# Scatter-adding expert rows straight into the output, and the order of the last block in a graph and mixture-of-experts layer

## The chip, the cores and the metric

The kernel runs on one NeuronCore of a Trainium2 chip. The metric is the device time of one execution in microseconds (us), given as the median of several runs. A core has a matrix engine (TensorE, PE in the profile, with its weight loads shown as PEld), a vector engine (DVE), a scalar engine (ACT), GpSimd (POOL) and a sync engine (SP) that here only issues DMAs. They run their own instruction streams and meet at semaphores. SBUF is the on-chip memory, PSUM holds matrix results.

## The reference

The layer takes 3125 nodes with 256 features and 50,000 edges. Its steps are:

```
xn  = layernorm(x)
gate = sigmoid(silu(edge_attr @ W1 + b1) @ W2 + b2)          # per edge
aggr = segment_sum(gate * xn[src], dst)                       # per node
x1  = x + xn + silu([xn, aggr] @ U1 + c1) @ U2 + c2 + linear_attention(xn)
probs = softmax(layernorm(x1) @ gate_w + gate_b)              # 16 experts
top 2 experts a node, weights divided by their sum
out = x1 + sum over a node's 2 experts e of
        weight * (silu(xn2 @ w1[e]) * (xn2 @ w2[e])) @ w3[e]  # xn2 = layernorm(x1), hidden 512
```

All tensors are float32. The change touches only the last line: the sum of the expert results onto `x1`.

## The kernel before

The first 797 us compute `x1` (kept in SBUF as tile `x`) and the routing. The rest is the expert stage. The 6250 pairs of node and expert are sorted into blocks of 256 slots, each block with one expert (`SB = 256`, at most `CAPB = 40` blocks). How many blocks there are is known only at run time. With this input there are 32, numbered 0 to 31, so `end`, read by `last_pair`, is 15. The 32 blocks have 8192 slots, and 1942 of them hold no pair. Such a spare slot has a destination row from `NP` = 3200 on, which is past the 3125 rows of the output.

Matrix products are done to nearly full float32 precision by splitting each operand into a high and a low half and adding three products (`PARTS`). ACT makes the high half (`w_high` for weights, `hid_high` for the hidden layer), DVE the low half (`w_low`, `hidden_low`). `ws[r]` holds both halves of weight `r`: 0 and 1 are the two column halves of w1 and w2 together, 2 is w3. There is one such pair for each `r`, so a new block's weights can be split only after the matrix engine has finished with the old ones. The raw weights have two buffers (`wst[r][p]`, with `p` the parity of the block), which SP fills in `load_w`.

For block `i` the work is:

- POOL gathers 256 rows of `xn2` (`gather_slots`, L648, two indirect DMAs of 128 rows);
- PE transposes them (`turn`), and computes the first layer in two halves: `expert_up(i, p, 0)` and `expert_up(i, p, 1)` (L1755, 24 matmuls each);
- for each half ACT applies silu (`silu_g`), DVE multiplies (`hidden`, L1442), ACT copies the high half (`hid_high`, L890), DVE makes the low half (`hidden_low`);
- PE computes the second layer, `expert_down(i, p)` (L1767, 24 matmuls);
- ACT scales by the slot weight and copies to `ys[p]` (`copy_y`, L897, two halves; it raises `s_y`);
- POOL adds the rows to a DRAM array (`scatter_slots`): it copies the block's destination rows to `idx[p]` (L657) and issues two indirect DMAs with `compute_op=ALU.add` (L661, 128 rows each). Since two blocks may hold the same node, a block's scatter waits until the one before has landed (`s_yst[1 - p]`).

The scatters go to `acc_d` (`out_rows` in the profile), with 3200 rows for nodes and 256 for spare slots. SP stores `x1` there in five chunks as its tiles are made, and one more copy that initializes the 256 spare rows. At the very end SP waits for all scatters and copies 3125 rows from `acc_d` to the output (L483).

The order on PE is software-pipelined by hand. In the loop, the first layer of the next block stands between the first and second layer of this one, and loop passes for pairs that don't exist are skipped by `If`. After the loop, blocks 30 and 31 remain in part. PE runs these three steps after the first half of block 31's first layer: second layer of 30, second half of the first layer of 31, second layer of 31. ACT and DVE follow the same order in their `block_steps`. POOL gathers four blocks ahead of its scatters, and after its loop four scatters remain (blocks 28 to 31).

Of the kernel before, what the change touches and what calls it, by code (L numbers as in the profile page):

```python
# [20 lines left out]
f32 = mybir.dt.float32  # L21
# [3 lines left out]
ALU = mybir.AluOpType  # L25
# [3 lines left out]
P = 128  # L29
N, D, E, RB = 3125, 256, 50000, 64  # L30
DC = D // P
NT = -(-N // P)
NP = NT * P
LAST = N - (NT - 1) * P
# [12 lines left out]
SB = 256  # L47
# [27 lines left out]
def ds(start, size):  # L75
    return bass.ds(start, size)
# [29 lines left out]
def gps_layer(nc, x_d, src_d, dst_d, first_d, rbf_d, W1_d, b1_d, W2_d, b2_d, U1_d, c1_d, U2_d, c2_d,  # L106
# [2 lines left out]
    XW = D + 2  # L109
    xn2_d = nc.dram_tensor("xn2_rows", (NP, XW), f32).ap()  # L110

    acc_d = nc.dram_tensor("out_rows", (NP + SB, D), f32).ap()

    ctx = ExitStack()
    with ctx:
# [32 lines left out]
        x = sb("x_nodes", [P, NT, D])  # L148
# [44 lines left out]
        ws = [[part(fr, 1024 * (2 * r + k), 4, D) for k in range(2)] for r in range(3)]  # L193
# [16 lines left out]
        idx = [sb(f"idx{i}", [P, ET], i32) for i in range(2)]  # L210
# [50 lines left out]
        dest = part(hgx, 128 + NS, NS).bitcast(i32)  # L261
# [7 lines left out]
        wst = [[part(big, 1024 * (2 * r + i), 4, D) for i in range(2)] for r in range(3)]  # L269
# [5 lines left out]
        ys = [part(xfl, 3072 + 512 * i, 2, D) for i in range(2)]  # L275
# [42 lines left out]
        s_turn = sem("gather_turn")  # L318
# [60 lines left out]
        s_acc = sem("x1_stored")  # L379
# [8 lines left out]
        def _(sp):  # L388
# [52 lines left out]
            for v in range(NB):  # L441
                for t in range(*XN2AT.get(v, (0, 0))):
                    store_xn2(t)
                for t0, end in CHUNKS:
                    if (end - 1) // 2 == v:
                        sp.wait_ge(s_x1, v + 3)
                        sp.dma_start(acc_d[t0 * P:end * P, :].rearrange("(t p) d -> p t d", p=P), x[:, t0:end, :])\
                            .then_inc(s_acc, 16)
                        if t0 == 0:
                            sp.dma_start(acc_d[NP:, :].rearrange("(t p) d -> p t d", p=P), x[:, 0:SB // P, :])\  # L450
                                .then_inc(s_acc, 16)
            for t in range(*CHUNKS[-1]):
                store_xn2(t)

# [25 lines left out]

            for p in range(2):
                sp.wait_ge(s_yst[p], 32 * end + 32)
            sp.dma_start(out_d[:, :], acc_d[0:N, :]).then_inc(s_out, 16)  # L483
            sp.wait_ge(s_out, 16)


        @block.gpsimd
        def _(pool):
# [161 lines left out]


            def scatter_slots(i, jp, p):
                pool.wait_ge(s_y, i + 3)
                if not (type(i) is int and i == 0):
                    pool.wait_ge(s_yst[1 - p], (jp + p) * 32)
                pool.wait_ge(s_tabi, 2)
                pool.tensor_copy(idx[p][:, 2:4], dest[:, ds(i * 2, 2)]).then_inc(s_didx, 1)  # L657
                pool.wait_ge(s_tabi, 2)
                pool.wait_ge(s_didx, i + 3)
                for s in range(2):  # L660
                    pool.indirect_dma_start(acc_d[:, :], bass.IndirectOffsetOnAxis(idx[p][:, 2 + s:3 + s], 0),  # L661
                                            ys[p][:, s, :], None, compute_op=ALU.add).then_inc(s_yst[p], 16)
            pool.sem_inc(s_didx, 2)
            for i in range(4):
                gather_slots(i, i % 2)
# [19 lines left out]
        def _(act):  # L685
# [184 lines left out]
            def w_high(r, i, j, p, first=False):  # L870
                act.wait_ge(s_win[r][p], (j + 1) * (32 if r < 2 else 16))

                if not first:
                    act.wait_ge(*((s_h, i * 4 + 4 + 2 * r + 2) if r < 2 else (s_o, i + 2)))
                act.copy(ws[r][0], wst[r][p]).then_inc(s_wh[r], 1)  # L875
# [11 lines left out]
            def hid_high(i, p, q):  # L887
                act.wait_ge(s_hid, i * 2 + q + 3)
                act.wait_ge(s_o, i + 1)
                act.copy(hids[p][0][:, 2 * q:2 * q + 2, :], hidf[q]).then_inc(s_hdh, 1)  # L890
# [8 lines left out]
                last.then_inc(s_y, 1)  # L899


            def block_steps(i, j, p, jn, last=False):
                silu_g(i, 0)
                if not last:
                    w_high(0, i + 1, jn, 1 - p)
                    slots_high(i + 1, 1 - p)
                hid_high(i, p, 0)
                w_high(2, i, j, p, first=(type(i) is int and i == 0))
                if not (type(i) is int and i == 0):
                    copy_y(i - 1, jn - 1, 1 - p)  # L910
                silu_g(i, 1)
                hid_high(i, p, 1)
                if not last:
                    w_high(1, i + 1, jn, 1 - p)
# [19 lines left out]
        def _(dve):  # L934
# [486 lines left out]

            dve.sem_inc(s_hid, 2)
            dve.sem_inc(s_xlo, 1)
            def w_low(r, i, p):
                dve.wait_ge(s_wh[r], i + 1)
                dve.tensor_tensor(ws[r][1], wst[r][p], ws[r][0].bitcast(f32), ALU.subtract).then_inc(s_wlo[r], 1)  # L1426

            def slots_low(i, p):
                dve.wait_ge(s_xhi, i + 1)
# [21 lines left out]
            def block_steps(i, p, last=False):  # L1451
                hidden(i, p, 0)
                if not last:
                    w_low(0, i + 1, 1 - p)
                    slots_low(i + 1, 1 - p)
                    slot_weights(i + 1, 1 - p)
                hidden_low(i, p, 0)
                w_low(2, i, p)
                hidden(i, p, 1)
                hidden_low(i, p, 1)  # L1460
                if not last:
                    w_low(1, i + 1, 1 - p)
# [19 lines left out]
        def _(pe):  # L1482
# [263 lines left out]
            def expert_up(i, p, q):  # L1746
                pe.wait_ge(s_wlo[q], i + 1)
                pe.wait_ge(s_xlo, i + 2)

                pe.wait_ge(s_hid, i * 2 + q + 1)  # L1750
                for m in range(2):
                    for k in range(2):
                        for c in range(DC):
                            for a, b in PARTS:
                                last = mm(ps[:, 2 * m + q, k * SB:(k + 1) * SB],  # L1755
                                          ws[q][a][:, 2 * m + c, k * P:(k + 1) * P], xTs[p][b][:, c, :],
                                          start=c == 0 and (a, b) == PARTS[0], stop=c == DC - 1 and (a, b) == PARTS[-1])
                    last.then_inc(s_h, 1)

            def expert_down(i, p):  # L1760
                pe.wait_ge(s_wlo[2], i + 1)
                pe.wait_ge(s_hdl, i * 2 + 2)
                pe.wait_ge(s_y, i + 1)
                for s in range(2):
                    for k in range(HC):
                        for a, b in PARTS:
                            last = mm(ps[:, 4 + p, s * D:(s + 1) * D], hids[p][a][:, k, s * P:(s + 1) * P],  # L1767
                                      ws[2][b][:, k, :],
                                      start=k == 0 and (a, b) == PARTS[0], stop=k == HC - 1 and (a, b) == PARTS[-1])
                last.then_inc(s_o, 1)  # L1770
            turn(0, 0, 0)
# [5 lines left out]
            with pe.Fori(0, CAPB // 2 - 1) as j:  # L1777
                with pe.If(end > j):
# [6 lines left out]
                    expert_down(j * 2 + 1, 1)  # L1785
                    expert_up(j * 2 + 2, 0, 1)
            expert_up(end * 2 + 1, 1, 0)
            expert_down(end * 2, 0)
            expert_up(end * 2 + 1, 1, 1)
            expert_down(end * 2 + 1, 1)  # L1790


# [35 lines left out]
```

## Time and profile before

| What | Value |
| --- | --- |
| median of 3 runs | 1130.9 us (1129.13 to 1131.05) |
| the profiled execution: its own time | 1130.0 us |
| its span, from first to last instruction | 1128.2 us |
| mean granted TensorE clock, as a share of full speed | 0.957 |
| chain of waits over the whole span, largest shares | POOL 39%, PE 37% |
| busy share of PE, DVE, ACT, POOL | 92%, 79%, 61%, 66% |
| expert stage, from the first first-layer matmul | 809.8 us to the end |

The profile page gives busy time by engine, the span in slices, the DMA queues, the chain of work that ended last, and groups of instructions by line. Times are from the start of the span. A row of a timeline has the start, the duration, engine and line, operation, what it writes `<-` what it reads, and in brackets the idle time of its engine before it with what ended that idle time. A DMA issued by POOL is shown for the time in which POOL generates it. When its data has landed is told apart, as time "to landing" from the start of the issue. SPq is SP's queue.

### The profile page before, as it was taken

The numbers are of one execution on the slowest core, as the hardware profiler recorded it, in microseconds if no ns is written. First come the engines' busy times: TensorE is split into PE (matmuls) and PEld (weight loads), VectorE is DVE, ScalarE is ACT, GpSimd is POOL, SyncE is SP. The second block draws the span as 40 slices with busy tenths as digits, with TensorE's granted clock in tenths as the row PEclk, the third lists the DMA queues.
The fourth block names the chain that finished last, engine by engine and source line by source line (L and its number), as shares of the span: only waits on it lengthen the run. The fifth ranks groups of instructions, "written<-read, shape, count | busy, mean of one in ns | idle before, by whom it ended". The sixth has DMA issues, their size and how long they took to land.

```text
span 1128.2 us, 23398 instructions
## 1 busy us (share of the span) xinstructions
PE 1033.9 (92%) x7884; PEld 978.0 (87%) x7884; DVE 889.9 (79%) x1411; ACT 686.0 (61%) x1055; POOL 746.6 (66%) x703
## 2 busy tenths in 40 slices
PE   4897999999999999999999999983499999999992
PEld 2466899999999999999999989983399999999991
DVE  7877998888999888888888843688487777777760
ACT  2562767766666666666666635652266777767760
POOL 5447877777777777777777756510267777767752
PEclk9998999999999999999999999985599999999996
DMA  7211444444444444444444401230678999888855
GB/s 241 77 53 42 135 146 143 143 141 141 143 143 142 140 141 141 143 143 141 141 141 143 125 26 56 85 104 1 178 215 226 230 235 226 237 233 235 227 119 137
DMA packets 118921, 165.25 MB, mean 146 GB/s; under 512 B 18625, under 2 KB 91382, under 8 KB 118774
## 3 DMA queue, kind: packets, MB, share of 16 engines
q1 hardware_dynamic: 87174, 95.14, 26.1%
q0 software_dynamic: 31104, 68.26, 25.3%
q8 instruction: 48, 0.79, 0.3%
q10 hardware_dynamic: 560, 0.79, 0.2%
q14 instruction: 35, 0.29, 0.1%
HBM read 145.62 MB, written 21.71 MB: 148 GB/s over the span
## 4 chain that ended last, share of the span: by engine, by line
POOL 39%; PE 37%; issue 13%; DVE 7%; DMA 2%; ACT 0%; POOLq 0%; DVEq 0%; ACTq 0%; SPq 0%
POOL big L590 19%; POOL hgx L590 19%; PE ps L1755 16%; PE ps L1767 8%; PE ps L1629 3%; PE ps L1502 2%; PE ps L1641 2%; PE ps L1654 2%; PE ps L1742 1%; PE ps L1668 1%; DVE st L961 1%; PE ps L1511 1%; PE ps L1512 1%; DMA hgx<-xn_rows,hgx 1%; PE ps L1495 1%
## 5 line engine op out<-in xcount | busy, mean ns | idle before, releaser
L1574 PE MATMUL ps<-fr 128*128 128x256 f32 x2352 | 306.9, 287 | 3.2 <-DVE fr L1023 3.2
L1574 PEld LDWEIGHTS ps<-fr 128*128 128x128 f32 x2352 | 289.4, 192 | 4.1 <-DVE fr L1023 4.0
L590 POOL DMA_INDIRECT big<-xn_rows,srcs x200 | 221.1, 1105 | 61.3 <-issue 61.3
L590 POOL DMA_INDIRECT hgx<-xn_rows,srcs x192 | 210.9, 1098 | 58.5 <-issue 58.5
L740 ACT ACTIVATE h1f<-ps,b 128x512 f32<-128x512 f32 x196 | 124.0, 684 | 165.5 <-PE ps L1528 164.3
L1585 PEld LDWEIGHTS ps<-oh,big 128*128 128x128 f32 x1568 | 189.8, 191 | 8.8 <-DVE big L1159 0.6
L1755 PE MATMUL ps<-fr 128*128 128x256 f32 x1536 | 192.0, 285 | 2.7 <-issue 1.4
L1755 PEld LDWEIGHTS ps<-fr 128*128 128x128 f32 x1536 | 188.6, 194 | 3.3 <-issue 1.8
L1585 PE MATMUL ps<-oh,big 128*128 128x96 f32 x1568 | 188.2, 273 | 0.5 <-DVE big L1168 0.5
L1023 DVE TENSOR_TENSOR fr<-h1f,fr 128x1024 fp32r<-128x1024 f32 x98 | 120.1, 1225 | 50.6 <-ACT fr L743 50.5
L661 POOL DMA_INDIRECT out_rows<-xnT,idx x64 | 115.4, 1803 | 35.6 <-POOL idx L657 24.2
L1426 DVE TENSOR_TENSOR fr<-big,fr 128x1024 fp32r<-128x1024 f32 x96 | 117.4, 1223 | 23.3 <-ACT fr L875 23.3
L875 ACT CAST fr<-big 128x1024 fp32r<-128x1024 f32 x96 | 100.7, 1049 | 51.9 <-PE ps L1767 37.3
L1145 DVE TENSOR_TENSOR big<-ps,b2bc 128x1024 f32<-128x1024 f32 x98 | 119.2, 1216 | 1.3 <-PE ps L1574 1.0
L1528 PE MATMUL ps<-fr 128*128 128x512 f32 x392 | 107.7, 396 | 1.9 <-DVE fr L1018 1.9
L747 ACT ACTIVATE big<-big 128x1024 f32<-128x1024 f32 x98 | 103.6, 1057 | 8.9 <-DVE big L1145 8.9
L743 ACT CAST fr<-h1f 128x1024 fp32r<-128x1024 f32 x98 | 102.6, 1047 | 8.5
L1767 PE MATMUL ps<-fr 128*128 128x256 f32 x768 | 101.3, 289 | 2.7 <-issue 2.3
L1767 PEld LDWEIGHTS ps<-fr 128*128 128x128 f32 x768 | 95.5, 194 | 3.1 <-issue 2.5
L648 POOL DMA_INDIRECT hgx<-xn_rows,idx x56 | 62.5, 1117 | 31.4 <-POOL idx L644 22.5
L1528 PEld LDWEIGHTS ps<-fr 128*128 128x128 f32 x392 | 67.6, 190 | 11.0 <-DVE fr L1018 2.1
L1018 DVE TENSOR_TENSOR fr<-rbf,fr 64x512 fp32r<-64x512 f32 x98 | 68.3, 698 | 3.1 <-DVE big L1120 0.2
(215 smaller groups left out, 1372.6 us busy)
## 6 DMA issues: line engine op xcount, KB each, us to landing
big<-in_w SPq DMA_DIRECT2D x128, 256.0 KB, 4.3
rbf<-in_rbf SPq DMA_DIRECT2D x98, 256.0 KB, 2.9
big<-in_w SPq DMA_DIRECT2D x32, 512.0 KB, 4.3
xn_rows<-xn SPq DMA_DIRECT2D x26, 128.0 KB, 2.4
big<-xn_rows,srcs POOLq DMA_INDIRECT x200, 3.1
out<-out_rows SPq DMA_DIRECT2D x1, 3125.0 KB, 11.9
xn_rows<-hgx SPq DMA_DIRECT2D x24, 128.0 KB, 2.2
hgx<-xn_rows,srcs POOLq DMA_INDIRECT x192, 3.1
```

The lines of the kernel that those rows point to most:

```text
L590: pool.indirect_dma_start(hg[i % HB][:, s, :], None, xn_d[:, :], bass.IndirectOffsetOnAxis(srcs[:, col:col + 1], 0))\
L661: pool.indirect_dma_start(acc_d[:, :], bass.IndirectOffsetOnAxis(idx[p][:, 2 + s:3 + s], 0), ys[p][:, s, :], None, compute_op=ALU.add).the ...
L740: act.activation(h1f[:, m, :], ps[:, m, :], ACT.Silu, bias=b1[:, m:m + 1]).then_inc(s_silu, 1)
L747: act.activation(th[p], th[p], ACT.Tanh, scale=0.5).then_inc(s_th, 1)
L1023: dve.tensor_tensor(h1s[p][1], h1f[:, :, :], h1s[p][0].bitcast(f32), ALU.subtract).then_inc(s_hlo, 1)
L1145: dve.tensor_tensor(th[p].rearrange("p (b s) d -> p b (s d)", b=2), ps[:, 2 + 4 * p:4 + 4 * p, :], b2bc[:, :, :].rearrange("p s d -> p (s ...
L1426: dve.tensor_tensor(ws[r][1], wst[r][p], ws[r][0].bitcast(f32), ALU.subtract).then_inc(s_wlo[r], 1)
L1528: last = mm(ps[:, m, :], W1s[k][:, m * P:(m + 1) * P], rbs[p], start=k == 0, stop=k == 1)
L1574: last = mm(ps[:, 2 + 4 * p + s // 2, (s % 2) * D:(s % 2 + 1) * D], h1s[p][a][:, c, s * P:(s + 1) * P], W2s[b][:, c, :], start=c == 0 and ...
L1585: last = mm(ps[:, 4 + p, c * w_n:(c + 1) * w_n], msg[p][:, s, c * P:(c + 1) * P], oh[p][:, s, 0:w_n], start=s == 0, stop=s == ET - 1)
L1755: last = mm(ps[:, 2 * m + q, k * SB:(k + 1) * SB], ws[q][a][:, 2 * m + c, k * P:(k + 1) * P], xTs[p][b][:, c, :], start=c == 0 and (a, b) ...
L1767: last = mm(ps[:, 4 + p, s * D:(s + 1) * D], hids[p][a][:, k, s * P:(s + 1) * P], ws[2][b][:, k, :], start=k == 0 and (a, b) == PARTS[0], ...
```

## The change

The array `acc_d` goes away. `x1` is stored straight to the output, the last chunk in two DMAs, because the last tile has only 53 valid rows. The scatters add into the output and carry a row limit, `bounds_check=N - 1` with `oob_is_err=False`, so a row for a spare slot is not written. The closing copy is gone; SP ends after its waits. In `scatter_slots` the copy of the destination rows stands ahead of the waits, and an extra `sem_inc(s_turn, 1)` stands between waits and DMAs. In the last block, w3 is split into the buffers of `ws[0]` (`w3_high`, and `w_low` with `to=0`), which are free after the first half of the first layer. PE runs the whole first layer of block 31, then the second layer of 30, then that of 31. ACT copies the result of block 30 after all hidden work of block 31.

```
@@ SP
-                        sp.dma_start(acc_d[t0 * P:end * P, :]..., x[:, t0:end, :])\
+                        full = min(end, NT - 1)
+                        sp.dma_start(out_d[t0 * P:full * P, :]..., x[:, t0:full, :])\
                             .then_inc(s_acc, 16)
-                        if t0 == 0:
-                            sp.dma_start(acc_d[NP:, :]..., x[:, 0:SB // P, :])\
-                                .then_inc(s_acc, 16)
+                        if end == NT:
+                            sp.dma_start(out_d[full * P:N, :], x[0:LAST, full, :]).then_inc(s_acc, 16)
...
-            sp.dma_start(out_d[:, :], acc_d[0:N, :]).then_inc(s_out, 16)
-            sp.wait_ge(s_out, 16)
+            sp.sem_inc(s_out, 1)
+            sp.wait_ge(s_out, 1)
@@ POOL
             def scatter_slots(i, jp, p):
+                pool.wait_ge(s_tabi, 2)
+                pool.tensor_copy(idx[p][:, 2:4], dest[:, ds(i * 2, 2)]).then_inc(s_didx, 1)
+                pool.wait_ge(s_tabi, 2)
                 pool.wait_ge(s_y, i + 3)
                 if not (type(i) is int and i == 0):
                     pool.wait_ge(s_yst[1 - p], (jp + p) * 32)
-                pool.wait_ge(s_tabi, 2)
-                pool.tensor_copy(idx[p][:, 2:4], dest[:, ds(i * 2, 2)]).then_inc(s_didx, 1)
-                pool.wait_ge(s_tabi, 2)
                 pool.wait_ge(s_didx, i + 3)
+                pool.sem_inc(s_turn, 1)
                 for s in range(2):
-                    pool.indirect_dma_start(acc_d[:, :], ..., ys[p][:, s, :], None, compute_op=ALU.add)
+                    pool.indirect_dma_start(out_d[:, :], ..., ys[p][:, s, :], None, bounds_check=N - 1,
+                                            oob_is_err=False, compute_op=ALU.add)
@@ ACT
+            def w3_high(i, j, p):
+                act.wait_ge(s_win[2][p], (j + 1) * 16)
+                act.wait_ge(s_h, i * 4 + 10)
+                act.copy(ws[0][0], wst[2][p]).then_inc(s_wh[2], 1)
...
                 hid_high(i, p, 0)
+                if last:
+                    w3_high(i, j, p)
+                    silu_g(i, 1)
+                    hid_high(i, p, 1)
+                    copy_y(i - 1, jn - 1, 1 - p)
+                    return
@@ DVE
-            def w_low(r, i, p):
+            def w_low(r, i, p, to=None):
+                halves = ws[r if to is None else to]
                 dve.wait_ge(s_wh[r], i + 1)
-                dve.tensor_tensor(ws[r][1], wst[r][p], ws[r][0].bitcast(f32), ALU.subtract)...
+                dve.tensor_tensor(halves[1], wst[r][p], halves[0].bitcast(f32), ALU.subtract)...
...
-                w_low(2, i, p)
+                w_low(2, i, p, to=0 if last else 2)
@@ PE (expert_down reads ws[r])
             expert_up(end * 2 + 1, 1, 0)
+            expert_up(end * 2 + 1, 1, 1)
             expert_down(end * 2, 0)
-            expert_up(end * 2 + 1, 1, 1)
-            expert_down(end * 2 + 1, 1)
+            expert_down(end * 2 + 1, 1, r=0)
```

## Rows read from the trace of the kernel before

**Rows 1.** chain of waits, PE's `turn` in two blocks, 27 blocks apart: start, us

```profile
830.70 0.44 PE ps L1742 x4
...
1075.68 0.44 PE ps L1742 x4
```

**Rows 2.** PE, ACT and DVE timelines, blocks 30 and 31, idle before in brackets

```profile
1093.70 1.23 DVE L1426 TENSOR_TENSOR fr<-big,fr 128x1024 fp32r<-128x1024 f32 x1 [0.26 <-ACT fr L875]
...
1096.20 0.62 ACT L890 CAST fr<-xnT 128x512 fp32r<-128x512 f32 x1 [1.56 <-DVE xnT L1442]
...
1098.07 3.04 PE L1755 MATMUL ps<-fr 128*128 128x256 f32 x24
...
1099.22 0.83 ACT L897 ACTIVATE xnT<-ps,hgx 128x256 f32<-128x256 f32 x2
...
1103.40 4.59 PE L1767 MATMUL ps<-fr 128*128 128x256 f32 x24 [2.29 <-issue]
...
1108.13 0.84 ACT L897 ACTIVATE xnT<-ps,hgx 128x256 f32<-128x256 f32 x2 [5.55 <-PE ps L1767]
```

**Rows 3.** POOL timeline, blocks 30 and 31

```profile
1102.07 0.19 POOL L657 COPY idx<-hgx 128x2 int32 x1 [2.47 <-issue]
1102.99 1.74 POOL L661 DMA_INDIRECT out_rows<-xnT,idx  x1 [0.74 <-POOL idx L657]
1105.04 1.54 POOL L661 DMA_INDIRECT out_rows<-xnT,idx  x1 [0.30 <-issue]
1109.30 0.18 POOL L657 COPY idx<-hgx 128x2 int32 x1 [2.71 <-ACT xnT L897]
1110.22 1.55 POOL L661 DMA_INDIRECT out_rows<-xnT,idx  x1 [0.74 <-POOL idx L657]
1112.08 1.54 POOL L661 DMA_INDIRECT out_rows<-xnT,idx  x1 [0.30 <-issue]
```

**Rows 4.** SP timeline: start, us, engine, line, operation, out<-in

```profile
753.23 0.37 SPq L447 DMA_DIRECT2D out_rows<-x_nodes  x1
757.48 0.81 SPq L440 DMA_DIRECT2D xn_rows<-xn  x2
...
1081.36 0.37 SPq L470 DMA_DIRECT2D big<-in_w  x1
1115.90 0.61 SPq L483 DMA_DIRECT2D out<-out_rows  x1
```

**Rows 5.** what SP's queue waited for, 780 to 1130 us: total, times, longest

```profile
SPq L482 <- DMA out_rows<-xnT,idx: 31.7, 1, 31.7
...
SPq L115 <- DMA out<-out_rows: 11.3, 1, 11.3
```

**Rows 6.** windows: busy of PE, PEld, DVE, ACT, POOL; granted clock, DMA

```profile
1101.00:1103.40 2.40, 0.11 (x1) 0.03 (x1) 1.38 (x2) 0.62 (x1) 0.59 (x2) 1.00 0.12 18
1103.40:1106.00 2.60, 2.60 (x14) 2.60 (x15) 0.00 (x0) 0.00 (x0) 2.29 (x2) 0.60 0.29 26
```

**Rows 7.** DVE and POOL timelines, a gather that follows waits without a copy

```profile
809.76 0.16 DVE L1437 TENSOR_REDUCE hgx<-hgx 128x2 f32<-128x4 f32 x1
...
810.69 1.26 POOL L648 DMA_INDIRECT hgx<-xn_rows,hgx  x1 [7.42 <-DVE hgx L1437]
```

**Rows 8.** line 661's 64 scatters: duration ns min/median/max; landing

```profile
L661 POOL DMA_INDIRECT out_rows<-xnT,idx x64: 1542/1616/2407, 830.9 to 1112.1; - x64
...
DMA to landing us min/median/max: 3.7/4.5/6.2
```

**Rows 9.** line 648's gathers: duration ns min/median/max

```profile
L648 POOL DMA_INDIRECT hgx<-xn_rows,idx x56: 947/1127/1461, 827.3 to 1076.2; - x56
```

**Rows 10.** POOL lines, 830 to 1079 us (27 blocks): busy, mean ns | idle

```profile
L661 POOL DMA_INDIRECT out_rows<-xnT,idx x54 | 98.1, 1818 | 30.3 <-POOL idx L657 20.4 <-issue 9.9
L648 POOL DMA_INDIRECT hgx<-xn_rows,idx x54 | 60.4, 1119 | 30.3 <-POOL idx L644 21.7 <-issue 8.0 <-DMA out_rows<-xnT,idx 0.6
...
L657 POOL COPY idx<-hgx 128x2 int32 (+1 forms) x28 | 16.0, 572 | 7.1 <-DMA out_rows<-xnT,idx 6.8
```

More of the change, by code:

```diff
@@ L110, in gps_layer @@
     xn2_d = nc.dram_tensor("xn2_rows", (NP, XW), f32).ap()
-    acc_d = nc.dram_tensor("out_rows", (NP + SB, D), f32).ap()
     ctx = ExitStack()
@@ L446, in _ @@
                         sp.wait_ge(s_x1, v + 3)
-                        sp.dma_start(acc_d[t0 * P:end * P, :].rearrange("(t p) d -> p t d", p=P), x[:, t0:end, :])\
+                        full = min(end, NT - 1)
+                        sp.dma_start(out_d[t0 * P:full * P, :].rearrange("(t p) d -> p t d", p=P), x[:, t0:full, :])\
                             .then_inc(s_acc, 16)
-                        if t0 == 0:
-                            sp.dma_start(acc_d[NP:, :].rearrange("(t p) d -> p t d", p=P), x[:, 0:SB // P, :])\
-                                .then_inc(s_acc, 16)
+                        if end == NT:
+                            sp.dma_start(out_d[full * P:N, :], x[0:LAST, full, :]).then_inc(s_acc, 16)
             for t in range(*CHUNKS[-1]):
@@ L655, in scatter_slots @@
                     pool.wait_ge(s_yst[1 - p], (jp + p) * 32)
-                pool.wait_ge(s_tabi, 2)
-                pool.tensor_copy(idx[p][:, 2:4], dest[:, ds(i * 2, 2)]).then_inc(s_didx, 1)
-                pool.wait_ge(s_tabi, 2)
                 pool.wait_ge(s_didx, i + 3)
+                pool.sem_inc(s_turn, 1)
                 for s in range(2):
-                    pool.indirect_dma_start(acc_d[:, :], bass.IndirectOffsetOnAxis(idx[p][:, 2 + s:3 + s], 0),
-                                            ys[p][:, s, :], None, compute_op=ALU.add).then_inc(s_yst[p], 16)
+                    pool.indirect_dma_start(out_d[:, :], bass.IndirectOffsetOnAxis(idx[p][:, 2 + s:3 + s], 0),
+                                            ys[p][:, s, :], None, bounds_check=N - 1, oob_is_err=False,
+                                            compute_op=ALU.add).then_inc(s_yst[p], 16)
             pool.sem_inc(s_didx, 2)
@@ L1423, in _ @@
             dve.sem_inc(s_xlo, 1)
-            def w_low(r, i, p):
+            def w_low(r, i, p, to=None):
+                halves = ws[r if to is None else to]
                 dve.wait_ge(s_wh[r], i + 1)
-                dve.tensor_tensor(ws[r][1], wst[r][p], ws[r][0].bitcast(f32), ALU.subtract).then_inc(s_wlo[r], 1)
+                dve.tensor_tensor(halves[1], wst[r][p], halves[0].bitcast(f32), ALU.subtract).then_inc(s_wlo[r], 1)
             def slots_low(i, p):
@@ L1758, in expert_up, with expert_down @@
                     last.then_inc(s_h, 1)
-            def expert_down(i, p):
+            def expert_down(i, p, r=2):
                 pe.wait_ge(s_wlo[2], i + 1)
@@ L1767, in expert_down @@
                             last = mm(ps[:, 4 + p, s * D:(s + 1) * D], hids[p][a][:, k, s * P:(s + 1) * P],
-                                      ws[2][b][:, k, :],
+                                      ws[r][b][:, k, :],
                                       start=k == 0 and (a, b) == PARTS[0], stop=k == HC - 1 and (a, b) == PARTS[-1])
```

## The prediction

> **What bounds the kernel now.** I read the chain of waits first, because the change touches only the end of the kernel and the expert loop. From 822 us to 1082 us it is PE alone: matmuls with no gap, (1075.68 − 830.70) / 27 = 9.07 us a block [rows 1]. Nothing that frees ACT, DVE, POOL or the DMA queues inside that loop can shorten it. It can only be lengthened. So the gain is in the tail, and I read the timelines there.
>
> The tail has three pieces. First, PE finishes block 31, with a gap of 2.29 us before its second layer and then a second layer of 4.59 us [rows 2]. Second, POOL scatters blocks 30 and 31, one after the other, since each waits for the last to have landed [rows 3]. Third, SP issues the closing copy at 1115.90 [rows 4], waits 11.3 us for it [rows 5], and the span ends at 1128.2. SP was done with its weight loads at 1081.36 [rows 4] and then only waited for scatters, 31.7 us [rows 5]. The closing copy hides behind nothing, and nothing hides behind it.
>
> **The closing copy.** From its issue to the end of the span is 1128.2 − 1115.90 = 12.3 us. Of this, 0.61 + 11.3 = 11.9 us are issue and transfer, and 0.4 us is the end of the program, which stays. Two instructions on SP's queue come instead; I take 0.1 us for them. Net −11.8 us.
>
> **The order of the last block.** The new order makes the result of block 31 earlier and that of block 30 later. Now, PE starts the second half of block 31's first layer at 1098.07, after the second layer of 30 [rows 2]. In the new order the two are swapped. One set of 24 matmuls lasts 3.04 us, so the half would start about 1095.0 to 1095.2. Its weights are split just in time: DVE does that at 1093.70 for 1.23 us, to 1094.93 [rows 2]. Then the second layer of 30 runs 1098.07 to 1101.11, without a wait, because its hidden layer was made before. ACT's `copy_y(30)` takes 0.14 to start (as 1108.13 follows 1107.99) and 0.84 us. So y(30) is ready at 1102.1, against 1099.22 + 0.83 = 1100.05 now.
>
> For block 31, the chain that is now the 2.29 us gap (silu, product, high half, low half) starts when its half ends, at 1098.07, instead of 1101.11. In front of it now stands the split of w3 into `ws[0]`: ACT follows the copy of 1096.20 + 0.62 [rows 2] with 1.05 us, then DVE needs 1.23 us, to about 1099.1, which holds the product up by some 0.6 us. Hidden work ends at 1098.07 + 2.29 + 0.6 = 1101.0, and the second layer of 31 can follow at 1101.1 to 1101.3. If the two splits stood in full ahead of it, it would be 1102.6. The gap on PE shrinks from 2.3 us to 0.1 to 1.5.
>
> The granted clock was 1.00 while PE idled in that gap, and 0.60 in the window that followed [rows 6]: mostly the lower level of 1.2 GHz, reached after the idle time. Full speed gives 24 matmuls in 3.04 us, the lower level took 4.59. Without the gap I expect 3.04, and y(31) at 1101.2 + 3.04 + 0.14 + 0.84 = 1105.2. With the late start and the low clock it is 1108.2. Both are compared below with what POOL can take. Its w3 load was issued at 1081.36 [rows 4] and is there long before.
>
> **The scatter of the last two blocks.** Now the order is: release, copy 0.18, 0.74 idle, first DMA, 1.86 to 2.05 us later the second, landing. ACT ends y(31) at 1108.97 and the DMA starts at 1110.22 [rows 3]: 1.25 us. With the copy ahead of the waits, the nearest row is a gather that follows waits and a semaphore increment only: DVE ends at 809.92, the DMA starts at 810.69 [rows 7], 0.77 us. So a link gains 0.5 us. From the start of the second DMA of block 31 to SP's issue is 1115.90 − 1112.08 = 3.8 us, near the least landing of 3.7 [rows 8].
>
> In the new kernel, with the generation unchanged:
>
> - y(30) 1102.05, + 0.77 = 1102.8 first DMA of 30 (block 29 was landed before 1102.07 even now [rows 3]);
> - + 2.05 (1105.04 − 1102.99) = 1104.9 second DMA, + 3.8 = 1108.7 landed;
> - y(31) is ready by 1105.2, by 1108.2 at the worst, so the landing is what comes last;
> - + 0.77 = 1109.4 first DMA of 31, + 1.86 = 1111.3 second, + 3.8 = 1115.1 landed, against 1115.9 now.
>
> That is −0.8 us. So of the 3.5 us by which y(31) comes earlier, little arrives: the pair of scatters behind y(30) becomes the bound, and y(30) is 2 us later. The PE clock of the last layer no longer counts.
>
> **The row limit and the spare slots.** 1942 of 8192 rows, 24%, are no longer moved. In the loop this unloads the DMA engines and nothing waits for that. In the tail, by the reference's own inputs, expert 15 has 107 pairs in one block and block 30 holds 163. If blocks are filled from the front, the second DMA of block 31 is empty and that of block 30 moves 35 rows. A landing of an empty DMA is in no row. It can gain nothing, or it can land with its sister: the first DMA of 31 starts 1.86 us earlier, so 1.9 us is the most that block 31 gives. I take 0.7 for both blocks, less than half of that, as the fixed part of the 3.8 stays. The Trainium skill ("DMA: Bandwidth & Descriptors", section "Anatomy of one DMA — SWDGE (gpsimd) path") fits 2.0 us plus bytes over 436 GB/s for each DMA, most of the fixed part being the receipt of the write. By it, an estimate, 128 KB fewer save only 0.3 us, and the forecast would come out 0.4 us later.
>
> What the limit costs POOL in generating a DMA is in no row either. Gathers take 0.95 us at least and scatters 1.54 [rows 8, 9]; the longest scatter is 2.41 [rows 8]. I bound the limit's effect d by −0.6 (rows dropped are rows not generated, down to a gather) and +0.87 (as the longest), and take 0, nearest to the typical 1.62. Four DMAs stand in the tail's chain behind y(30), so 4d: −2.4 to +3.5 us.
>
> In the loop POOL has per block two gathers, two scatters, two copies and the idle time between. At their least these are 2 × 1.54 + 2 × 0.95 + 2 × 0.18 + 2 × 0.78 + 2 × 0.30 = 7.5 us of 9.07 [rows 3, 8, 9]. Of the 1.6 us left, only 7.1 us over 27 blocks, 0.26 a block, shows as idle time that ends with a landing; the rest is in lengthened copies (572 ns against 180) and DMAs (1818 against 1542) [rows 10]. So a d up to 0.13 is covered for certain, up to 0.78 perhaps. The moved copy helps here: where the scatter waits for a landing, it now starts 0.5 us sooner. `sem_inc(s_turn)` adds an instruction of POOL's queue, below 0.1 us, covered the same way. Behind a waiting scatter stand the next gather, for which PE's `turn` waits, and the next scatter, for which `copy_y` waits.
>
> **Stores of x1.** The extra DMA on SP stands behind the one at 753.23 and before `xn2` stores at 757.48 [rows 4]. It takes about 0.4 us in a gap of 3.9. The early copy of the spare rows is gone, off the path. Both 0.
>
> **Sum.** −11.8 − 0.8 − 0.7 = −13.3 us. The profiled execution would take 1130.0 − 13.3 = 1116.7. The median of the runs shown is 0.9 above it, so the forecast is 1117.6 us.
>
> **Rivals.**
>
> A. *The scatter chain doesn't get shorter.* The wait with its increment costs the same 1.25 us as the copy did, and empty DMAs land as full ones. Then y(30) at 1102.05 gives 1103.3, landed 1109.2, 1110.4, landed 1116.1: 0.2 us later than now. Total −11.6: 1119.3 us. For it: the landing depends little on rows in the window where the queue is idle. Against it: the row of the gather [rows 7].
>
> B. *Dropped rows make generation shorter.* The tail's DMAs with few rows are built in the time of a gather or less; 4 × −0.6 = −2.4 on top: 1115.2 us. For it: a scatter takes 0.6 us longer than a gather, so its time depends on the work per row. Against it: nothing shows that a skipped row is free.
>
> C. *The row limit makes POOL the bound of the loop (slower).* Each scatter DMA is built 2d longer per block. PE then waits at `turn` or, through `copy_y`, at its second layer. With d = 0.87 (each as the longest in the trace) and half of the uncertain cover, 0.9 us a block, the loop loses 27 × (1.74 − 0.9) = 22.7 us and the tail 3.5. With −13.3 that makes +12.9: 1143.8 us. It decides from 4d + 27 × (2d − 0.9) = 13.3, that is d = 0.65 us. For it: POOL is the engine with the least visible slack next to PE in this stage [rows 10]. Against it: the whole work for 128 rows of an accumulating scatter takes 1.54 to 1.62 us [rows 8], and one comparison a row should be a small part of that. The Trainium skill speaks for it ("GPSIMD Engine Reference", section "Elementwise — side-by-side cycle accounting"): a branch that depends on data costs about 12 cycles an element, at the 1.2 GHz of its example 10 ns. For 128 rows that would be an estimate of 1.28 us a DMA, and the kernel would come to about 1168 us. No run here shows it.
>
> D. *It doesn't do what it says in the last block*: the first half of layer one frees `ws[0]` late or ACT queues w3's split behind a wait. Then y(30), which ACT copies after all hidden work of 31, slips too. The worst above, 1102.6 for the hidden work, puts y(30) at 1103.4 instead of 1102.1: 1.3 us, 1118.9 us. It lies in the forecast's range.
>
> **How the numbers follow.** Forecast with D: 0.67. A 0.12, B 0.12, C 0.09. The forecast goes with the likeliest, 1117.6. Downward, B's 4d with the full 1.2 us more from empty DMAs reaches 1114; upward, d = +0.87 in the tail with the loop still covered gives 1121.1. The range is 1114.0 to 1121.5. It leaves out C, and a little on each side. What a measurement of this kernel can tell from no change is about 0.2%, 2.3 us. A, B and the forecast are all faster by far more; C is slower, unless d lies within some 0.04 us of its turning point. Faster 0.89, same 0.02, slower 0.09.
>
> **What would show it.** After the change, the page has no out<-out_rows copy, and the span ends within about 0.6 us of the last landing. In the loop PE's period stays 9.07 us with no gap before `turn`. L661's median stays near 1.6 us: 1.0 speaks for B, above 2.3 for C. On PE the gap before the last second layer is below 1.5 us, and the granted clock there stays near 1.00. POOL's first DMA of block 31 starts about 0.8 us after a landing and not after ACT. If it follows ACT, y(31) was later than I say. The prediction is wrong if the loop's period grows, or if the time between y(30) and the last landing isn't 12 to 13 us.

## The result

The kernel after takes 1117.5 us (median of 4 runs, 1116.67 to 1119.88), the kernel before 1131.0 us in the same comparison. The ratio is 0.9888, with a 95% interval of 0.9868 to 0.9907, so 10.5 to 14.9 us less. Compared once more (label e11_after_third), it took 1117.0 against 1130.3 us, ratio 0.9883 (0.9867 to 0.9900). The forecast was 1117.6 us.

The profiled execution of after has a span of 1118.1 us and is the longest of the four. The page's list of busy times, first of before, then of after, has the same work on PE, DVE and ACT:

```profile
PE 1033.9 (92%) x7884; PEld 978.0 (87%) x7884; DVE 889.9 (79%) x1411; ACT 686.0 (61%) x1055; POOL 746.6 (66%) x703
PE 1034.4 (93%) x7884; PEld 978.7 (88%) x7884; DVE 890.0 (80%) x1411; ACT 686.4 (61%) x1055; POOL 747.4 (67%) x703
```

In the group list the scatter now writes `out`. Its mean over all blocks is 1860 ns, where before had 1803. That is no effect of the change: before has 1773 in a second trace, after 1794 and 1841, and e4, which has no row limit, 1903. Its least time is unchanged:

```profile
L661 POOL DMA_INDIRECT out_rows<-xnT,idx x64 | 115.4, 1803 | 35.6 <-POOL idx L657 24.2
L661 POOL DMA_INDIRECT out<-xnT,idx x64 | 119.0, 1860 | 49.2 <-issue 34.4
```

```profile
L661 POOLq MOVE  x64: 29/29/38, 832.5 to 1111.2; - x64
L661 POOL DMA_INDIRECT out<-xnT,idx x64: 1542/1576/2397, 833.3 to 1113.3; - x64
```

The chain of waits has PE's `turn` in two blocks 27 apart, as [rows 1] had: (1077.89 − 832.91) / 27 = 9.07 us a block.

```profile
832.91 0.44 PE ps L1756 x4
...
1077.89 0.44 PE ps L1756 x4
```

Single executions differ ahead of the expert loop: its first `turn` starts at 809.55 us in this trace of after and at 805.33 in another (e11). So I measure the tail from one fixed event, the last `turn` of the loop (block 31's). It starts at 1084.59 in before and at 1086.80 in after. From there to the end of the span it is 43.6 us in before and 1118.1 − 1086.80 = 31.3 us in after: 12.3 us less. Two more traces of after have 31.3 each, a second one of before has 43.9. On the clock of after, where 2.2 us are to be taken off to compare with [rows 2, 3], PE runs this:

```profile
1086.80 0.60 PE L1756 MATMUL ps<-ident,hgx 128*128 128x128 f32 x4
...
1094.43 6.01 PE L1769 MATMUL ps<-fr 128*128 128x256 f32 x48 [1.28 <-DVE xnT L1456]
1100.28 6.14 PE L1781 MATMUL ps<-fr 128*128 128x256 f32 x48
```

The last 24 matmuls follow the ones of block 30 with 0.2 us between, and end at 1106.4. ACT copies both results:

```profile
1098.94 1.04 ACT L907 CAST fr<-big 128x1024 fp32r<-128x1024 f32 x1
...
1103.54 0.84 ACT L898 ACTIVATE xnT<-ps,hgx 128x256 f32<-128x256 f32 x2 [1.04 <-PE ps L1781]
1106.56 0.84 ACT L898 ACTIVATE xnT<-ps,hgx 128x256 f32<-128x256 f32 x2 [2.19 <-PE ps L1781]
```

POOL's timeline of blocks 30 and 31 answers to [rows 3]. The copies of the index rows (L653) now lie behind the DMA before them and not ahead of the next:

```profile
1099.98 1.28 POOL L653 COPY idx<-hgx 128x2 int32 x1
1105.26 1.56 POOL L661 DMA_INDIRECT out<-xnT,idx  x1 [3.99 <-ACT xnT L898]
1107.13 1.54 POOL L661 DMA_INDIRECT out<-xnT,idx  x1 [0.30 <-issue]
1108.10 0.77 POOL L653 COPY idx<-hgx 128x2 int32 x1
1111.45 1.55 POOL L661 DMA_INDIRECT out<-xnT,idx  x1 [2.58 <-DMA out<-xnT,idx]
1113.31 1.54 POOL L661 DMA_INDIRECT out<-xnT,idx  x1 [0.31 <-issue]
```

Block 31's first scatter waits for a DMA, not for ACT, though y(31) is ready at 1106.56 + 0.84 = 1107.4. And there is something that the prediction does not have. The instructions of the last line of the program's frame (L114) say when each engine ends; the columns are duration in ns and start in us:

```profile
L114 ACTq DRAIN  x1: 739/739/739, 1106.7 to 1106.7; - x1
L114 POOLq DRAIN  x1: 6128/6128/6128, 1111.7 to 1111.7; - x1
...
L114 SPq DRAIN  x1: 13/13/13, 1116.2 to 1116.2; - x1
```

SP is through its waits, and the last scatter has landed, before 1116.2. POOL's closing drain lasts until 1111.7 + 6.13 = 1117.8, which is 3.0 us after its last scatter was generated (1113.31 + 1.54 = 1114.85), and the span ends 0.3 us later, at 1118.1. In before the same drain hid behind the closing copy:

```profile
L115 POOLq DRAIN  x1: 6264/6264/6264, 1110.4 to 1110.4; - x1
...
L115 SPq DRAIN  x1: 13/13/13, 1128.0 to 1128.0; - x1
```

### The profile page after: what moved, and what is told of

Its sections match the earlier page's. It is cut to its first block, busy times and chain, and to the rows that moved or that the text cites. A ratio compares the mean times of both kernels' runs of the same rounds, so it can differ in the third digit from the quotient of the medians.

```text
span 1118.1 us, 23447 instructions
## 1 busy us (share of the span) xinstructions
PE 1034.4 (93%) x7884; PEld 978.7 (88%) x7884; DVE 890.0 (80%) x1411; ACT 686.4 (61%) x1055; POOL 747.4 (67%) x703
## 4 chain that ended last, share of the span: by engine, by line
PE 85%; DVE 9%; issue 2%; DMA 2%; ACT 1%; DVEq 0%; POOL 0%; POOLq 0%; SPq 0%; ACTq 0%
PE ps L1588 25%; PE ps L1769 16%; PE ps L1599 15%; PE ps L1542 8%; PE ps L1781 8%; PE ps L1643 3%; PE ps L1516 2%; PE ps L1655 2%; PE ps L1668 2%; PE ps L1756 1%; PE ps L1682 1%; DVE st L974 1%; PE ps L1525 1%; DMA hgx<-xn_rows,hgx 1%; PE ps L1526 1%
## 5 line engine op out<-in xcount | busy, mean ns | idle before, releaser
L589 POOL DMA_INDIRECT big<-xn_rows,srcs x200 | 218.8, 1094 | 61.3 <-issue 61.3
L661 POOL DMA_INDIRECT out<-xnT,idx x64 | 119.0, 1860 | 49.2 <-issue 34.4
L647 POOL DMA_INDIRECT hgx<-xn_rows,idx x56 | 59.9, 1070 | 32.0 <-POOL idx L643 22.9
```

The costliest lines, as they stand in the source:

```text
L589: pool.indirect_dma_start(hg[i % HB][:, s, :], None, xn_d[:, :], bass.IndirectOffsetOnAxis(srcs[:, col:col + 1], 0))\
L661: pool.indirect_dma_start(out_d[:, :], bass.IndirectOffsetOnAxis(idx[p][:, 2 + s:3 + s], 0), ys[p][:, s, :], None, bounds_check=N - 1, oob ...
```

## The experiments

All kernels are judged by two numbers: the time against before, and in the trace the time from the last `turn` to the end (T). T is what tells parts of 1 us apart; before has 43.6 and after 31.3. In two of the comparisons (e5 to e7, and e8 to e10) every kernel, before included, was about 100 us slower, on other chips and in the edge stage alone (the expert stage's first `turn` comes at 907.9 us in e8, at 807.2 in before); those medians are compared only within their own group, and T is not touched.

**e1_direct_only.** The direct scatter alone, in the old order and with the copy of the indices behind the waits.

```
 before +
-  acc_d = nc.dram_tensor("out_rows", ...)       # scatters and x1 go to out_d, with bounds_check=N - 1
...
-  sp.dma_start(out_d[:, :], acc_d[0:N, :])
```

> The kernel before with the direct scatter-add alone (output as target, row limit, no closing copy); the last block's order and the place of the index copy are those of before. Theory (the parts add up, and the program now ends with POOL's drain, which in the trace of after runs until 3.0 us past the last generated scatter): last scatter ends as before at 1113.6, end of span 1113.6 + 3.0 + 0.25 = 1116.9 against 1128.2, so 11.3 us less than before, about 1119.7 us. Rival 1 (the end follows the landing, as the prediction had it): 11.8 us less, and the span ends 0.4 us after the last landing. Rival 2 (the other two edits bring nothing): 13.4 less, 1117.5 us.

Measured: 1118.7 us against 1130.4, ratio 0.990 (0.9885 to 0.9915), T = 1116.3 − 1084.44 = 31.9. So 11.7 us come from this part. The end is POOL's drain again, as the theory said:

```profile
L114 POOLq DRAIN  x1: 6128/6128/6128, 1109.9 to 1109.9; - x1
...
L114 SPq DRAIN  x1: 13/13/13, 1114.4 to 1114.4; - x1
```

The drain ends at 1109.9 + 6.13 = 1116.0, and SP was free at 1114.4. Rival 1 had the right sum (11.8) for a wrong reason: its end, 0.4 us after the landing, would have been about 1114.8. The theory's own 11.3 was 0.4 short, because PE's last second layer ran at full clock here, so that the scatter of block 31 started 0.5 us earlier than in before (25.2 us after the last `turn`, not 25.6). That half microsecond goes with the clock, and no run shows that the edit sets the clock.

**e2_order_only.** The new order of the last block alone, on before.

```
 before +
   expert_up(end * 2 + 1, 1, 0)
+  expert_up(end * 2 + 1, 1, 1)
   expert_down(end * 2, 0)
-  expert_up(end * 2 + 1, 1, 1)
-  expert_down(end * 2 + 1, 1)
+  expert_down(end * 2 + 1, 1, r=0)              # and w3_high, w_low(to=0), copy_y order as in after
```

> The kernel before with the last block's new order on PE, ACT and DVE alone; scatters to the side array, closing copy kept, index copy behind the waits. Theory (scatter chain behind y(30) is the bound): the last landing moves by +0.2 us, time within 0.5 us of before, although PE ends about 3.5 us earlier. Rival (PE's end set the end of the kernel): 3 to 3.5 us faster than before.

Measured: 1129.7 us against 1130.4, ratio 1.000 (0.999 to 1.001), T = 1127.9 − 1084.49 = 43.4. PE ends its last matmul 3.8 us earlier than in before, 19.6 us after the last `turn` instead of 23.4, and the kernel gets only 0.2 us faster. The last landing was expected 0.2 us later. SP issues the closing copy 1115.32 − 1084.49 = 30.8 us after the last `turn`, where before had 1115.90 − 1084.59 = 31.3, so it came 0.5 us earlier, and the copy to the end of the span took 0.3 us longer. POOL's timeline shows why so little arrives: the first scatter of block 31 now waits for a DMA, where in before it waited for ACT [rows 3].

```profile
1101.22 0.84 ACT L897 ACTIVATE xnT<-ps,hgx 128x256 f32<-128x256 f32 x2 [1.05 <-PE ps L1780]
1104.24 0.84 ACT L897 ACTIVATE xnT<-ps,hgx 128x256 f32<-128x256 f32 x2 [2.17 <-PE ps L1780]
```

```profile
1102.24 0.18 POOL L657 COPY idx<-hgx 128x2 int32 x1 [5.50 <-ACT xnT L897]
1103.17 1.56 POOL L661 DMA_INDIRECT out_rows<-xnT,idx  x1 [0.74 <-POOL idx L657]
1105.04 1.54 POOL L661 DMA_INDIRECT out_rows<-xnT,idx  x1 [0.30 <-issue]
1108.89 0.18 POOL L657 COPY idx<-hgx 128x2 int32 x1 [2.32 <-DMA out_rows<-xnT,idx]
1109.82 1.55 POOL L661 DMA_INDIRECT out_rows<-xnT,idx  x1 [0.74 <-POOL idx L657]
1111.68 1.54 POOL L661 DMA_INDIRECT out_rows<-xnT,idx  x1 [0.30 <-issue]
```

**e3_copy_behind.** After, with the old place of the index copy.

```
 after, scatter_slots:
-  pool.tensor_copy(idx...) ahead of the waits; pool.sem_inc(s_turn, 1)
+  the waits, then pool.tensor_copy(idx...)
```

> The kernel after with the index copy back behind the waits and without the extra semaphore increment. Theory: two links of the chain (y(30) to its first DMA, landing of block 30 to the first DMA of block 31) take 1.25 us again in place of the 0.88 of after, so +0.7 us against after; in the loop nothing. Rival (the copy was hidden anyway): 0.

Measured: 1118.3 us, T = 1117.7 − 1085.91 = 31.8, 0.5 more than after. From ACT's end to the DMA it is 1104.70 − 1103.49 = 1.21 us, in after 0.88; from the start of block 30's second DMA to the first of 31 4.43, in after 4.32. The chain of waits parts the second link from the landing before it:

```profile
1107.13 3.44 DMA out<-xnT,idx
```

```profile
1106.56 3.22 DMA out<-xnT,idx
```

The first line is after, the second e3. From the landing to the DMA it is 1111.45 − 1110.57 = 0.88 us in after and 1110.99 − 1109.78 = 1.21 in e3. So each of the two links is 0.33 us longer here, as the theory said (0.7 for both), and a landing that was 0.2 us faster hides part of it; three more traces of the new order with the limit (e5, e9, e11) have 3.34 to 3.45 for that landing. The time alone can't tell it: 0.5 us is under 0.2% of it. The step from e1 to e3 is the new order: 31.9 to 31.8, of which the fast landing may be 0.2.

**e4_no_limit.** After, with scatters to a side array and no row limit. The sums are left out of the output.

```
 after, scatter_slots:                           # x1 is stored to out_d and to acc_d
-  pool.indirect_dma_start(out_d[:, :], ..., bounds_check=N - 1, oob_is_err=False, compute_op=ALU.add)
+  pool.indirect_dma_start(acc_d[:, :], ..., compute_op=ALU.add)
```

> The kernel after with the scatters to a side array of 3456 rows without a row limit, so that the spare rows move again. It leaves the sums out of the output (no closing copy); x1 is stored to both. Theory (end set by POOL's drain, which counts from generation): the landing of block 30 takes 3.8 us from its second DMA in place of 3.44, +0.4 us against after; the last landing comes 1.4 us later than in after but sets nothing. Rival (end follows the last landing): +1.4 us. Rival (limit costs generation time): L661 shortest durations fall below 1.54 us.

Measured: 1118.8 us, T = 1118.2 − 1086.77 = 31.4, 0.1 more than after.

```profile
L667 POOL DMA_INDIRECT out_rows<-xnT,idx x64: 1542/1576/2607, 833.1 to 1113.4; - x64
...
DMA to landing us min/median/max: 3.7/4.6/6.2
```

```profile
L115 POOLq DRAIN  x1: 6287/6287/6287, 1111.7 to 1111.7; - x1
...
L115 SPq DRAIN  x1: 13/13/13, 1117.4 to 1117.4; - x1
```

Three things follow. The generation of a scatter costs the same with and without the limit: 1542 ns at least and 1576 in the median in both. And SP is free only at 1117.4, 4.0 us after the last DMA's start at 1113.36, instead of 2.9 in after. So a scatter without rows does land 1.1 us earlier, but the end hardly moves, because POOL's drain sets it. And of the expected 0.4 us only 0.1 came, since two effects meet: the landing of block 30 takes 3.70 us here and 3.44 in after, but both links are shorter without the limit, 1105.14 − 1104.34 = 0.80 and 1111.50 − 1110.71 = 0.79 us in place of 0.88.

```profile
1107.01 3.70 DMA out_rows<-xnT,idx
```

**e5_pool_waits.** After, with POOL waiting for the landings before its program ends.

```
+  for p in range(2):
+      pool.wait_ge(s_yst[p], 32 * end + 32)     # at the end of POOL's program
```

> The kernel after with one more pair of waits at the end of POOL's program: for the landing of all scatters. Theory A (POOL's closing drain takes a fixed time after the last generated DMA, whatever POOL waits for in between): end of span unchanged. Theory B (the drain takes its some 3 us from where POOL's program ends): it starts at the last landing, 1.25 us later than the generation ends, and the span grows by 1.2 to 1.3 us. Theory C (the drain is bound to the landing): 0, and the drain is short, under 1.8 us.

Measured: T = 1228.2 − 1195.66 = 32.5, 1.2 more. This is theory B. The drain starts with SP's, at the landing, 1.4 us after the last generation ended (1222.06 + 1.54 = 1223.60), and still lasts 3.0 us. So it is not a wait for the DMAs. It ends 3.0 us after the last thing that POOL's program has to do, be that a generation (after, e1, e6) or a wait (e5). What POOL does in these 3.0 us no run shows. In time the kernel was 0.990 (0.986 to 0.994) of before, which doesn't separate 1.2 us. The execution of the trace took 1230.0 us, above the kernel's median of 1222.5, but in its tail the matmuls last as long as in after (6.01 and 6.14 us for 48).

```profile
L114 SPq DRAIN  x1: 13/13/13, 1225.0 to 1225.0; - x1
L114 POOLq DRAIN  x1: 3017/3017/3017, 1225.0 to 1225.0; - x1
```

**e6_one_scatter_less.** After, without the last scatter, which has no rows with this input.

```
-  for s in range(2):
+  for s in range(1):                            # in the last block alone, with a semaphore of its own
```

> The kernel after without the second scatter DMA of the last block, which carries no row with this input (its 107 pairs are all in the first). Theory (end = last generation + 3.0 us drain + 0.25): generation ends 1.86 us earlier, so -1.9 us against after. Rival (end follows the last landing): the first DMA of the block starts 1.86 us earlier but lands after 3.4 to 3.8 us in place of 2.8, so -0.9 to -1.3 us.

Measured: T = 1220.0 − 1190.50 = 29.5, 1.8 less than after. The drain ends 1215.0 + 4.79 = 1219.8, SP was free at 1219.2. The theory said 1.9, the rival 0.9 to 1.3. The end follows POOL's last generation, which ended at 1215.25 + 1.55 = 1216.8.

```profile
L114 POOLq DRAIN  x1: 4789/4789/4789, 1215.0 to 1215.0; - x1
...
L114 SPq DRAIN  x1: 13/13/13, 1219.2 to 1219.2; - x1
```

**e7_halves, e10_halves_again, e12_halves_third.** A version meant to beat after. The second layer of block 30 is cut in two, and its first scatter starts when its own 128 rows are copied. The first half goes to a free PSUM bank.

```
   expert_up(end * 2 + 1, 1, 0)
+  expert_down(end * 2, 0, part=range(1))        # rows 0 to 127, bank 6
   expert_up(end * 2 + 1, 1, 1)
-  expert_down(end * 2, 0)
+  expert_down(end * 2, 0, part=range(1, 2))     # rows 128 to 255
   expert_down(end * 2 + 1, 1, r=0)
```

> The kernel after with the second layer of block 30 in two halves of 12 matmuls, one before and one after the second half of block 31's first layer, and with the first scatter DMA of block 30 issued as soon as its own 128 rows are copied. Theory (the chain behind y(30) sets the end): first DMA of block 30 waits only for the landing of block 29, the second starts at 1105.4 in place of 1107.1 on the clock of after, and everything behind it moves by 1.7 us: -1.7 us against after, and y(31) at 1108.3 is still ahead of the landing of block 30. Rival (y(31) or the landing of block 29 becomes the bound): -0.5 us or nothing.

> The kernel with the second layer of block 30 in two halves, on the same chip as the kernel after. Theory (its first scatter of block 30 now waits for the landing of block 29): end of span less last turn of the loop 30.5 us, 0.8 less than after. Rival (the landing of block 29 was late only on the other chip, where the first timing was made): 29.6 us, 1.7 less.

> The version in halves once more. Its two traces differ by where block 29 had landed: 30.5 us from the last turn to the end where the landing came last, 29.05 where y(30) did. Theory: one of these two again, 0.8 to 2.3 us under its partner, told by whether the first scatter of block 30 starts 0.9 us after a landing or its second 0.9 us after ACT's second half. Rival (both traces were luck): 31.3.

T was 30.5, 29.1 and 29.1, against 31.3. In the first trace block 29's second scatter was issued at 1199.23, landed 4.26 us later, at 1203.49, and was the last thing that block 30's first scatter (1204.52) waited for. That is the rival's case: 0.8 less. In the two others y(30) is last. The third's timelines:

```profile
1101.08 0.47 ACT L912 ACTIVATE xnT<-ps,hgx 128x256 f32<-128x256 f32 x1
1105.04 0.84 ACT L906 ACTIVATE xnT<-ps,hgx 128x256 f32<-128x256 f32 x2 [3.48 <-PE ps L1797]
```

```profile
1094.36 1.82 POOL L669 DMA_INDIRECT out<-xnT,idx  x1 [0.30 <-issue]
...
1099.35 1.56 POOL L669 DMA_INDIRECT out<-xnT,idx  x1 [2.98 <-issue]
1102.41 1.54 POOL L669 DMA_INDIRECT out<-xnT,idx  x1 [1.50 <-ACT xnT L912]
...
1106.85 1.55 POOL L669 DMA_INDIRECT out<-xnT,idx  x1 [2.69 <-DMA out<-xnT,idx]
1108.70 1.54 POOL L669 DMA_INDIRECT out<-xnT,idx  x1 [0.30 <-issue]
```

The second scatter of block 30 starts at 1102.41, 18.0 us after the last `turn` (1084.43). In after it is 20.3. That is 2.3, more than the 1.7 that was expected. The second DMA no longer follows the first by 1.87 us, and besides y(30) is ready 0.5 us earlier, at 17.1 in place of 17.6, mostly because behind PE's last matmul of block 30 stands one half copy of 0.47 us and not two of together 0.84. In the third comparison, with its partner on the same chip, it took 1115.2 us (1113.36 to 1115.92), after 1117.0 (1116.06 to 1117.87). The ratios to before are 0.9861 (0.9844 to 0.9877) and 0.9883 (0.9867 to 0.9900). So it beats before in time, and after in the trace. In time it is 1.8 us below after here, with intervals that overlap. In the comparison before that (e10 and e9) the two can't be told apart: 0.9924 (0.9890 to 0.9959) and 0.9933 (0.9892 to 0.9973), with medians of 1219.8 and 1219.1 us. The first (e7) gave 0.986 (0.981 to 0.991) without a partner. That this version is faster than after is shown by T and not by the times.

**e8_before_again, e9_after_again, e11_after_third.** The two kernels unchanged.

> The kernel before, unchanged, against itself, to learn what two equal kernels differ by and whether the low clock in the last second layer comes back. Theory A (the fall belongs to the 2.29 us gap of PE ahead of it): the granted clock falls again inside the last 24 matmuls, 4.6 us. Theory B (it can fall or not with the same gap, as it did not with the direct scatter alone): the last second layer takes 3.1 us at clock 1.00 this time or 4.6 again, and the end of the span less the last turn of the loop stays within 0.7 us of 43.6 us.

> The kernel after, unchanged, on the same chip as the two others. Theory (parts: 11.7 direct, 0.5 copy ahead of the waits, 0.1 order): end of span less last turn of the loop 31.3 us again, 12.3 less than before, ratio to before 0.989. Rival (the 13.4 us of the first timing are real, and a part of the gain lies ahead of the expert stage): ratio 0.988 or less, with the expert stage starting earlier than in the trace of before.

> The kernel after once more, as the partner of the next one. Theory: end of span less last turn of the loop 31.3 us, as in its two other traces.

T of after is 31.3 in all three traces, T of before 43.9 (1229.6 − 1185.74) in the second. The last second layer of before took 4.51 us in that trace, after the same gap of 2.29 us. So in two of three traces with this gap the clock fell inside the last 24 matmuls. In e1, with the same gap, it did not, and they took 3.11. The windows of e1, the gap and the matmuls after it:

```profile
1100.94:1103.14 2.20, 0.02 (x1) 0.00 (x0) 1.37 (x2) 0.62 (x1) 0.75 (x2) 1.00 0.00 0
1103.14:1105.44 2.30, 2.19 (x18) 2.22 (x19) 0.01 (x1) 0.00 (x0) 2.00 (x2) 1.00 0.20 9
```

The granted clock (the column before the last two) is 1.00 in both, where before had 0.60 behind its gap [rows 6]. Where the gap was gone (after three times, e2 to e6) it was always 1.00, and so it was behind the gap of 0.86 us that the version in halves has (three traces). e8 against before gave 1.0015 (0.997 to 1.006), so on that chip nothing under half a per cent could be told. e9's 0.9933 (0.9892 to 0.9973) came from there. It stands for 3.3 to 13.3 us less, which holds the 12.3 of the traces.

## Why the prediction was right, and where it wasn't

The mechanism, the sign and the time were right. The sum was −13.3 us from the trace. The traces give −12.3, and the medians −13.4 and −13.3. The last 1 us of agreement is luck as far as the runs show: the interval of the first comparison reaches from −10.5 to −14.9 and that of the third from −11.3 to −15.0, both hold −12.3, and nothing in the tail accounts for more. On the way, in us after the last `turn`:

| Step | predicted | after |
| --- | --- | --- |
| y(30) ready | 17.5 | 17.6 |
| first, second scatter of 30 | 18.2, 20.3 | 18.5, 20.3 |
| y(31) ready | 20.6 | 20.6 |
| first, second scatter of 31 | 24.8, 26.7 | 24.7, 26.5 |
| end of the span | 30.3 | 31.3 |

Two of the prediction's own signs came out against it. The span was to end within about 0.6 us of the last landing and ends 1.9 after it. From y(30) to the last landing it was to be 12 to 13 us and is 1116.2 − 1104.38 = 11.8. The others held: no closing copy, 9.07 us a block, L661's median at 1.58 us, a gap below 1.5 us at clock 1.00, and the first scatter of block 31 behind a landing.

**The closing copy.** Taken at −11.8. The direct scatter alone gave −11.7 (e1), but that the two agree is luck. From the last landing to the end it was 12.3 us in before and is 1.9 in e1 and in after: −10.4. In e1 the other 1.35 us are an earlier landing (SP is free 30.0 us after the last `turn`, not 31.3), from the empty scatter and the clock. In after the landing comes 1.9 us earlier (29.4), where the sum had 0.8 + 0.7 = 1.5.

**The order of the last block.** The gap on PE went from 2.29 to 0.2 us, y(31) came 3.8 us earlier (so also by the prediction's own times, 1108.97 and 1105.2, beside which it says 3.5), and next to nothing of it arrived, as predicted (e2: −0.2; e1 to e3: −0.1). The scatter chain behind y(30) took over. That the clock falls because of the gap was only half right. With the gap it may fall or not; it didn't matter for after.

**The copy ahead of the waits.** The link was taken at 0.77 us from a gather. It is 0.88. The limit adds a register move (L661 POOLq MOVE above) and 0.1 us before a block's first scatter: the idle time between index copy and DMA is 0.84 in e1 and e3 and 0.74 in before and e2, and the link without the limit is 0.80 (e4). The copy's place was taken to bring 0.5 us in each of two links. It brings 0.33 in each (1.21 to 0.88, e3).

**The row limit.** The effect on generation, taken at 0 between −0.6 and +0.87, is 0 (e4). That rules out rivals B and C. The Trainium skill ("GPSIMD Engine Reference", section "Elementwise — side-by-side cycle accounting") has about 12 cycles an element for a branch that depends on data, from which rival C's estimate of 1.28 us a DMA came. The traces show nothing of it in this instruction: 1542 ns at least and 1576 in the median, with the limit and without.

**The spare rows, and the step that failed.** I took 0.7 us for scatters with few rows. The effect on the landings was there and larger than I took: 1.1 us for the empty one, and 0.3 on the landing of block 30 (3.70 in e4, 3.44 in after). The Trainium skill ("DMA: Bandwidth & Descriptors", section "Anatomy of one DMA — SWDGE (gpsimd) path") would have had 0.3 for 128 KB, an estimate by its bytes over 436 GB/s. The empty scatter saved 1.1 us, and that decides. But the last landing doesn't end the program, and here the sum failed. I took 0.4 us from landing to end, read off a program in which POOL had been done for 11 us. That term is 1.9 us in after (1118.1 − 1116.2), because POOL's drain lasts until 3.0 us after its last scatter is generated. It is 1.4 us more than the 0.5 in the sum; the last scatter started 0.2 us earlier and landed 0.2 us faster than summed, which leaves the 1.0 us by which the tail was missed. The row for it was in the trace of before, in POOL's last instructions, and I had read only SP's end.

**Rivals.** A (chain not shorter, 1119.3) was wrong in its 1.25 us for a link (0.88) and in its landings. In time alone it can't be told from the forecast: 1119.3 lies within the first interval. D (y(30) slips behind hidden work) did not occur: ACT was through with the hidden work of 31 at 1102.5 and then waited 1.04 us for PE's second layer of 30.

## What to carry to other kernels

Where a closing step is removed, what it hid becomes the end. List the last instruction of every engine, with its drain, before taking "last landing plus a little" for it. When a tail is a chain of scatters that wait for one another, the first of the last two blocks decides, so its result should be early, in pieces if need be; finishing the last block 3.8 us sooner brought 0.2 (e2). And a part that moves one engine by 4 us without moving the end is best measured from one fixed event in the trace, since the runs' own spread of 3 us would hide it.

## What the runs showed of the hardware

POOL's closing drain ends 3.0 us after its last indirect DMA has been generated, in after, e1 and e6 without POOL waiting for the landing (3.0 to 3.1 in before, e2 and e4 as well). Where POOL's program first waits for the landing, 1.4 us longer, the drain takes 3.0 us from there (e5). An accumulating scatter of 128 rows takes 1.54 us to generate, with all its rows dropped by a limit (after) or with none dropped (e4). From the start of a scatter with no rows left until SP goes on it is 2.9 us, of a full one 3.8 (before) to 4.0 (e4). The granted clock fell inside the last 24 matmuls after a gap of 2.29 us in two traces out of three, and took them from 3.1 to 4.5 and 4.6 us.
